# Two linear-mixture stages: some of the first block's scatters issued after the stage boundary, and one group of slot loads placed behind the eighth store

## The reference, cut to what matters

```python
def _moe_linear(x, router_w, expert_w):
    logits = x @ router_w.T
    vals, idx = jax.lax.top_k(logits, K)          # K = 2 of 8 experts
    probs = jax.nn.softmax(vals, axis=-1)
    ...
    for e in range(n_exp):
        out = out + combine[:, e:e + 1] * (x @ expert_w[e].T)
    return out
```

## Time and profile before

| what | us |
|---|---|
| median of 3 runs | 2659.98 |
| lowest and highest of them | 2646.7 and 2660.24 |
| profiled execution, its own time | 2658.76 |
| its span, first to last instruction | 2656.9 |
| PE busy | 2371.1 |
| DVE busy | 1639.1 |
| ACT busy | 1458.3 |
| POOL busy | 782.5 |

### The profile page before, as it was taken

One profiled execution on the slowest core, in us unless ns is written; L12 is line 12 of the kernel. 1 busy time (PEld: TensorE's weight loads), 2 busy tenths in 40 slices (PEclk: granted clock), 3 DMA queues, 4 the chain that ended last, 5 costly groups with the idle time before them and its releaser, 6 DMA issues. The chain is left out here.

```text
span 2656.9 us, 41487 instructions
## 1 busy us (share of the span) xinstructions
PE 2371.1 (89%) x13315; PEld 1219.7 (46%) x13402; DVE 1639.1 (62%) x2942; ACT 1458.3 (55%) x3263; POOL 782.5 (29%) x830
## 2 busy tenths in 40 slices
PE   7978999998797789999999998978998759998878
PEld 3445666665586222222222225874444544443333
DVE  5777988975332789999999842332445522444555
ACT  3572333333465478888888886655444337553344
POOL 1224665640233600000000002343543024442113
PEclk9988999998899799999999999998999879998899
DMA  5343223211375321021111003867666018665112
GB/s 163 87 145 121 86 92 107 90 37 42 110 215 158 91 31 32 10 41 20 24 26 16 4 5 122 275 197 269 225 216 208 1 58 308 220 202 141 27 31 74
DMA packets 206358, 287.34 MB, mean 108 GB/s; under 512 B 25168, under 2 KB 129104, under 8 KB 203408
## 3 DMA queue, kind: packets, MB, share of 16 engines
q1 hardware_dynamic: 187752, 234.80, 29.6%
q0 software_dynamic: 18432, 50.36, 6.1%
HBM read 176.04 MB, written 107.73 MB: 107 GB/s over the span
## 5 line engine op out<-in xcount | busy, mean ns | idle before, releaser
L3264 DVE TENSOR_REDUCE big<-psum 128x2 f32<-128x1024 f32 x512 | 602.6, 1220 | 70.5 <-PE psum L3052 68.3
L3216 ACT ACTIVATE probs<-psum 128x512 f32<-128x512 f32 x1024 | 554.8, 598 | 120.0 <-PE psum L3079 111.9
L3079 PE MATMUL psum<-big,k_ops 128*128 128x512 bf16 x946 | 291.8, 387 | 13.1 <-ACT probs L3216 11.0
L1735 PE MATMUL psum<-big,turned 128*128 x480 | 234.1, 616 | 16.8 <-ACT turned L1895 13.0
L1834 PE MATMUL psum<-big,probs 128*128 128x512 f32 x512 | 231.6, 603 | 6.1 <-DVE down_sum L2015 6.1
L3079 PEld LDWEIGHTS psum<-big,k_ops 128*128 128x128 bf16 x1024 | 80.8, 97 | 328.2 <-ACT probs L3216 258.2
L1429 ACT ACTIVATE hidden<-psum,big 128x128 f32<-128x128 f32 x480 | 136.2, 372 | 98.9 <-PE psum L1322 98.4
L644 POOL DMA_INDIRECT linear_rows<-desk_tokens,linear_row x128 | 124.6, 974 | 208.0 <-DVE linear_row L620 105.4
L1685 POOL DMA_INDIRECT big<-linear_y,linear_row x128 | 124.8, 975 | 203.8 <-PE psum L1735 128.6
L1903 ACT ACTIVATE big<-psum 128x512 f32<-128x512 f32 x240 | 139.9, 597 | 78.6 <-PE psum L1735 67.2
L3052 PE MATMUL psum<-big,w_A_or_L_A 32*128 32x512 bf16 x1024 | 159.9, 391 | 23.5 <-DVE big L3264 15.8
(11 more groups left out here) (505 smaller groups left out, 4004.5 us busy)
## 6 DMA issues: line engine op xcount, KB each, us to landing
linear_y<-big SPq DMA_DIRECT2D x240, 256.0 KB, 4.1
big<-in_experts SPq DMA_DIRECT2D x120, 322.0 KB, 3.9
big<-step_rows SPq DMA_DIRECT2D x16, 1024.0 KB, 4.7
qkv_chunks<-big SPq DMA_DIRECT2D x48, 256.0 KB, 2.3
big<-qkv_chunks SPq DMA_DIRECT2D x16, 768.0 KB, 4.5
big<-linear_rows SPq DMA_DIRECT2D x48, 256.0 KB, 3.9
big<-since_rows SPq DMA_DIRECT2D x32, 256.0 KB, 5.4
big<-row_store SPq DMA_DIRECT2D x32, 256.0 KB, 5.3
```

Source lines behind the costliest of these rows:

```text
L1735: pe.matmul(k.bank[bank_of(n, m)][:, :], turned[:, q % 2, t % 4, :], w["up" if r else "gate"][:, bass.ds(experts[r][t] * TB, TB)], start=T ...
L3079: pe.matmul(ring_bank(ring_at(i, m))[:, :], k_ops[:, g % 2, h, kt * P:(kt + 1) * P], q_ops[:, g % 2, i % QB, h, :], start=True, stop=True) ...
L3216: act.activation(probs[:, kt % 2, h, :], ring_bank(ring_at(i, m))[:, :], ACT.Exp, scale=SCALE).then_inc(expd.sem, 1)
L3264: dve.tensor_reduce(into, k.row_pair[hp].rearrange("p (h t) -> p h t", h=2), AX.X, ALU.max).then_inc(row_max.sem, 1)
```

## The change

In layer 1's feed-forward 9 of the 16 scatters of the linear stage's first block are issued (all eight of router 0 and one of router 1) instead of 16, and in the window attention 3. The linear stage issues the rest as GpSimd's first work, ahead of the left gathers and of block 1's scatters, with no wait for a tile. SyncE brings only router 0's slots of block 0 at the start; it issues the four loads of router 1 behind the eighth store (m = 7). The pacing of block 1's scatters is the formula that was in force before.

```diff
@@ sorted_silu_ffn, gpsimd
             if linear:
-                ahead.pool(pool, 4 * TPB, lambda step: reached(NB - 1, 7 + step // 2 - AHEAD))
+                ahead.pool(pool, 9, lambda step: reached(NB - 1, 7 + step // 2 - AHEAD))
@@ sorted_linear_ffn, sync
-            for r in range(ROUTERS):
-                bring_slots(0, r)
+            bring_slots(0, 0)
             for n in range(NB):
                 for m in range(TILES):
                     store(n, m)
+                    if n == 0 and m == 7:
+                        bring_slots(0, 1)
                     if n == 0 and m == 22:
                         bring_slots(1, 0)
@@ sorted_linear_ffn, gpsimd
-            late = begun.scattered < 4 * TPB
+            route.pool_scatter(pool, 0, begun.scattered, 4 * TPB)
             if left:
                 left.gather(pool, 0, TPB)
-            route.pool_scatter(pool, 0, begun.scattered, 4 * TPB, lambda step: at_tile(0, (step - 2 * TPB) * 5 // 4) if step >= 2 * TPB else None)
-            scatter(1, lambda step: at_tile(0, min(10 + step * 5 // 4, TILES - 1) if late else 4 + step * 8 // 5))
+            scatter(1, lambda step: at_tile(0, 4 + step * 8 // 5))
@@ window_attention, gpsimd
-            ahead.pool(pool, 4 * TPB)
+            ahead.pool(pool, 3)
```

## The result

The changed kernel's median is 2638.68 us (2635.41 to 2641.5), the kernel before beside it had 2657.5 us. The ratio is 0.9933 with a 95% interval of 0.992 to 0.9945: 18.8 us, or 0.7%, faster. Forecast were 2641.0 us and 18.9 us. Two later copies of the changed kernel gave 0.9943 (0.9926 to 0.996) and 0.993 (0.9914 to 0.9946) on their chips.

The account below looks back on a forecast made before the run. PE, busy 2371.1 of 2656.9 us, was taken to idle at two linear-stage openings, waiting for GpSimd's queue. Savings of 8.8 + 10.1 = 18.9 us from 2658.76 gave 2639.9; with the median 1.2 us higher, 2641, range 2630 to 2651.

Parts of the forecast that it names:

- the door: Stage end where all engines meet before the linear stage; claimed held by GpSimd's drain, 9.8 and 17.1 us behind the others.
- the tail: From the last early scatter's end to the end of GpSimd's drain: 5.3 us after layer 1's feed-forward, 1.4 to 2.0 elsewhere.
- the turn: PE's first work on slots in the linear stage (L1719); at the second opening forecast at 2171.5 against 2181.80.
- Opening A, 8.8 us: Linear stage's start after layer 1's feed-forward: seven fewer early scatters save 8.8 us, bounds 0 to 9.8.
- The rival with a tail that doesn't move: After layer 1's feed-forward nothing is gained; 10.1 us gained alone, time 2650, chance 0.09.
- Opening A, what is added at no cost: Seven scatters and four gathers run at the linear stage's start; block 1's scatters keep 2.7 us of cover, cost 0.
- Opening B, 10.1 us: Linear stage's start after the window attention: three early scatters instead of 16 save 10.1 us, bounds 9.5 to 10.3.
- the pattern: Opening ahead of layer 1's first feed-forward, three scatters early and five after: 11.1 us from the door to the turn.
- Router 1's loads, 0: In the linear stage, four loads moved between stores 7 and 8: PE waits 0 to 0.4 us per opening, taken as 0.
- rival 2: At both openings PE's slow clock or late loads give back 7 us: gain 12, time 2648, chance 0.12.
- The slower rival: At both openings GpSimd's drain ends at its own time, not with the scatters; 6.6 us lost, time 2667, chance 0.03.
- The rule against it: After the window attention, DVE's port hold could cost five scatters 0.23 us each, sum 17.7; left out.

Follow-up runs that it names:

- the copies on the second chip: Unaltered kernel before and unaltered changed kernel, rerun on the second chip: 2657.12 us (ratio 1.0001) and 2641.67 us (0.9943 against before).
- the added drain: Changed kernel plus one GpSimd drain ahead of the nine scatters in layer 1's feed-forward: 2642.89 us, ratio 0.9942 against the kernel before.
- loads first: Changed kernel with router 1's loads right behind router 0's, ahead of the first store: 2668.43 us, ratio 0.9959 against the kernel before (2677.07 us).
- the kernel behind store 12: Changed kernel with router 1's loads behind store 12 instead of store 7: 2651.88 us, ratio 0.9983 against the kernel before.
- The third chip's copy: Changed kernel, unaltered, run again on the third chip: 2636.41 us, ratio 0.993 against the kernel before.
- eight and eight: Changed kernel with 8 scatters issued early at both places instead of 9 and 3: 2633.21 us (0.9925 against before) on the second chip, 2637.28 us (0.9922) on the third.
- only A: Changed kernel with 16 scatters instead of 3 in the window attention, 9 kept in layer 1's feed-forward: 2676.29 us, ratio 1.0002 against before.

## Why the prediction was right, point by point

**The total.** Forecast 18.9 us, measured 18.8, with an interval of 14.6 to 21.3. That the two agree to 0.1 us is luck. That each opening came within 0.3 us of its own sum is luck only in part: at B the door, the tail and the turn came out one by one, at A two errors of about half a microsecond cancelled (below).

**Opening A, 8.8 us.** Measured 8.92 in the first comparison, 9.5 between the copies on the second chip. The door opened 16.32 us behind the first scatter instead of 25.24, and the way from door to turn stayed 4.53 us. The tail behind the ninth scatter's end was 4.7 us where I had kept 5.3. The rival with a tail that doesn't move falls: with 3, 8, 9 and 16 scatters the tail is 4.6, 4.7, 4.7 and 5.3 us. I had called it unexplained; with the added drain 3.1 of the 4.7 us went, so most of it is the backlog from the gathers.

**What the prediction lacks here is a condition.** The 9.8 us by which GpSimd was last came from one execution on one chip. On the first chip of the experiments, where layer 1's stage ended 12 to 14 us later behind the first of sixteen scatters, GpSimd was last by 0.5 us or not at all, and the medians show no gain from A's part. The 8.8 us is a price of the stage's end, not of the scatters. That the first comparison ran where the stage ended as in the trace of before was luck, which the chances did not count.

**Opening A, what is added at no cost.** Block 1's scatters started at 1802.58 after 1.53 us of idle time, where 2.7 us were estimated and 11.6 had been. They waited for DVE's places, not for GpSimd. Right, with 1.5 us of cover left.

**Opening B, 10.1 us.** Measured 10.34: the door 16.91 us sooner (16.9 forecast), the way from door to turn 11.11 us instead of 4.54 (11.1 forecast from the pattern), the tail 1.43 us (1.4 from the earlier trace rows), PE's wait 6.37 us (6.6). The pattern had the number because it was the same number of scatters on both sides of a door, and this step is the best of the forecast. Every profile with three scatters ahead of door B shows 16.0 to 16.2 us from the first one to the turn.

**Router 1's loads, 0.** PE's turns of that group, 1810.63 and 2181.78, have no DMA as releaser. The bound of 0 to 0.4 us was right but close: the cover is 0.25 us. On the third chip two profiles with the same loads waited 0.33 and 0.23 us at A, inside the bound too. ScalarE's wait for a store, forecast at 1 us, was 1.67 at A, covered by PE's lead (five products by the code, where the prediction wrote four banks):

```profile
1814.40 0.60 ACT L1903 ACTIVATE big<-psum 128x512 f32<-128x512 f32 x1 [1.67 <-DMA linear_y<-big]
```

One thing was missed. I called the removal of the four loads at the start worth nothing, and judged it by data that was there. With eight scatters of router 1 behind the door they would have held the first store for 4.6 us: "loads first" shows it. What that costs in time stays below what the medians resolve.

**The clock, rival 2.** It cost at most a fraction of the rival's 7 us. Windows of the changed kernel (granted clock before the DMA share):

```profile
1791.00:1797.00 6.00, 5.21 (x14) 2.97 (x13) 2.56 (x12) 3.14 (x5) 4.51 (x5) 0.52 0.31 113
1797.00:1803.00 6.00, 6.00 (x26) 3.51 (x25) 2.89 (x16) 3.99 (x8) 3.56 (x5) 1.00 0.66 227
...
2161.00:2167.00 6.00, 4.96 (x12) 2.91 (x13) 0.00 (x0) 2.32 (x3) 4.58 (x5) 0.50 0.57 191
2167.00:2173.00 6.00, 6.00 (x23) 3.39 (x23) 2.53 (x15) 3.52 (x8) 0.20 (x1) 0.85 0.37 145
```

In the kernel before the second window of A was at 0.87 and that of B at 0.96. From the first turn to that of router 1's second group it took 22.70 us at A (23.45 before) and 24.37 at B (23.07 before): -0.8 and +1.3 us, not the 7 of the rival. Between the copies on the second chip it was +0.7 and +0.6, so the gain at A isn't a steady one. Nor is the loss at B all clock: 0.5 of the 1.3 us had come by router 1's first turn, and the other 0.8 lie between its first and second group, where the granted clock was 1.00 (window 2179 to 2185) and PE stood for 0.57 us for something that the profile doesn't name. The rival's mechanism is real, as the kernel behind store 12 shows, where a pause fell into work at full clock. At both openings PE is at 0.50 to 0.52 in the first window after the turn, in the kernel before and in the changed one, so the new pause at B fell where the clock is low in both.

**The slower rival** falls with both drains: at B it lasted 5.2 us with three scatters, 11.7 with eight, 17.1 with sixteen.

**The rule against it.** Here the prediction drew a wrong sentence from one row. It said that the row disagrees with the port rule. The changed kernel's seventh scatter at A starts 0.60 us into the DVE multiplication of L1176 and lasts 1.44 us instead of 0.96 (its timeline is above). The third chip's copy, and then eight and eight on the second chip, same view:

```profile
1777.80 1.21 DVE L1176 TENSOR_TENSOR probs<-probs,desk_share 128x1024 f32<-128x1024 f32 x1
1778.11 1.74 POOL L644 DMA_INDIRECT linear_rows<-desk_tokens,linear_row  x1 [0.30 <-issue]
```

```profile
1776.74 1.22 DVE L1176 TENSOR_TENSOR probs<-probs,desk_share 128x1024 f32<-128x1024 f32 x1
1777.68 1.10 POOL L644 DMA_INDIRECT linear_rows<-desk_tokens,linear_row  x1 [0.30 <-PE psum L1322]
```

In all three the scatter ends 0.82 to 0.84 us behind the end of the multiplication: 1779.28 - 1778.45, 1779.85 - 1779.01, 1778.78 - 1777.96. The trace of before had it as well, further ahead, in layer 1's first feed-forward:

```profile
791.37 1.22 DVE L1176 TENSOR_TENSOR probs<-probs,desk_share 128x1024 f32<-128x1024 f32 x1
792.09 1.33 POOL L498 DMA_INDIRECT slot_rows<-desk_tokens,desk_row  x1 [0.30 <-PE psum L1322]
```

In the fourteen profiles 44 indirect DMAs start inside this instruction, and 43 of them end 0.82 to 0.83 us behind it; the other starts in its last 0.01 us and takes its usual 0.96. They wait for its end; the one that begins 0.01 us ahead of it, as in the earlier trace rows, runs through. The instruction isn't alone: of 118 that start inside DVE's multiplication of 128x512 at L2000, 117 end 0.81 to 0.90 us behind that one. I had read the one row that by its phase couldn't show the rule. The Trainium skill, "SBUF — State Buffer", section "SBUF: two separate sides", says that a VectorE operation in certain modes, or one with two SBUF inputs against a GpSimd operation that reads SBUF, holds the port pair that the two share for its whole length; that GpSimd can't write descriptors meanwhile it says of the modes. Both multiplications have two SBUF inputs, and the runs agree with the rule for them. Its size was small: 0.48 us lost beside a gain of 8.92, hidden in the forecast by the shorter tail. At B the rule's 1.2 us did not come: beside DVE's short operations the five scatters kept 1.26 us (2151.09 to 2156.14 in four steps).

## What to carry to other kernels

Work begun ahead of a stage's end is free only until the engine that is last without it; what is past that point costs its full length, so count instructions on both sides of the door. Which engine is last depends on what feeds the stage, and can differ from chip to chip; compute the gain against the next-latest drain, and look at more than one profile of it. When a producer moves behind the door, move its consumer's loads behind the stores too, and check the other end: a load that is too late costs its wait and then some, since TensorE's clock may fall in the pause.

## What was not expected of the hardware

- GpSimd's rows end sooner than GpSimd. A drain behind eight gathers of L1169 ended 5.8 us after the last one's row; behind three scatters alone the lag was 1.4 us, behind sixteen 1.9.
- A DVE multiplication of 128x1024 with two SBUF inputs holds back an indirect DMA of GpSimd that starts inside it: the DMA's row ends 0.82 to 0.83 us behind it in 43 of 44 meetings, and lasts up to 1.74 us instead of 0.96. So does one of 128x512 (117 of 118 within 0.81 to 0.90 us).
- A pause of 4.6 us in running work was followed by a window of 7 us at a granted clock of 0.51 at A, and of 0.76 at B; it cost 7.4 and 5.7 us.
- The kernel before took 2677 us on one chip and 2657 on two others, and from 1650 to 1750 us, in the stage fed by expert weights, the profiles there moved 253 to 265 GB/s against 273 to 286.

Open: what the gathers' backlog consists of; whether sixteen scatters ahead of door A lengthen the stage's end on the first chip; why "only A" on the first chip had 301.2 us from its first turn to the stage's end, where its neighbours had 291.5 to 295.2. It is spread over the stretch and has no wait that stands out, and may be no more than one execution.
